# A fold of the layer-1 sums placed behind the pair sums of its slot, in a recommender kernel on one Trainium2 core

## What the reference computes

```
z = einsum('bfe,bge->bfge', x, xk)            # x: embeddings, xk: x itself in layer 0
z = relu(einsum('bcl,oc->bol', z, Ws[i]) + bs[i])
z = sum(z, axis=-1)                           # 16 numbers for a sample
xk = broadcast(z)                             # so layers 1 and 2 need only z of the layer before
```

## Time and profile before

| | before |
|---|---|
| median of 3 runs | 556.3 us (556.26 to 556.32) |
| the profiled execution's own time | 556.66 us |
| its span in the trace | 554.5 us |
| instructions in the span | 17,864 |
| granted TensorE clock | 1.0 of full speed throughout |

### The profile page before, as it was taken

One profiled execution on the slowest core, in us unless ns is written; L12 is line 12 of the kernel. 1 busy time (PEld: TensorE's weight loads), 2 busy tenths in 40 slices (PEclk: granted clock), 3 DMA queues, 4 the chain that ended last, 5 costly groups with the idle time before them and its releaser, 6 DMA issues.

```text
span 554.5 us, 17864 instructions
## 1 busy us (share of the span) xinstructions
PE 525.8 (95%) x7472; PEld 300.4 (54%) x7472; DVE 516.9 (93%) x257; ACT 416.6 (75%) x1208; POOL 459.3 (83%) x533
## 2 busy tenths in 40 slices
PE   2778889999999999999999999999999999999997
PEld 1334544655555565555556555555655555565465
DVE  4799999999999999999999999999999999999763
ACT  3476877878878687887868788786878878687743
POOL 6999898898998989898898989989898999987200
PEclk9999999999999999999999999999999999999999
DMA  3822333332323333232333323233332333332000
GB/s 91 221 77 68 94 90 91 89 83 70 92 83 87 88 82 85 69 98 78 81 90 83 87 69 102 74 86 90 79 87 70 89 85 84 90 82 77 1 2 2
DMA packets 40263, 45.03 MB, mean 81 GB/s; under 512 B 27124, under 2 KB 27508, under 8 KB 40184
## 3 DMA queue, kind: packets, MB, share of 16 engines
q0 software_dynamic: 12288, 33.57, 21.9%
q1 hardware_dynamic: 27896, 10.33, 7.8%
HBM read 42.58 MB, written 1.29 MB: 79 GB/s over the span
## 4 chain that ended last, share of the span: by engine, by line
PE 69%; issue 10%; ACT 9%; DVE 9%; DMA 1%; SPq 1%; POOL 1%; ACTq 0%; DVEq 0%; POOLq 0%
PE sum_ps L693 30%; PE outer_ps L768 9%; PE turn_ps L671 9%; PE outer_ps L799 8%; DVE prods L243 7%; PE sum_ps L708 4%; ACT relu_k L546 4%; PE outer_ps L778 4%; ACT relu L535 2%; PE outer_ps L814 2%; ACT emb_t L508 1%; DMA emb<-tables,rows_sb 1%; ACT h L553 1%; POOL emb L309 1%; PE outer_ps L708 1%
## 5 line engine op out<-in xcount | busy, mean ns | idle before, releaser
L243 DVE TENSOR_TENSOR prods<-turn_ps,emb_t 128x3136 f32<-128x3136 f32 (+3 forms) x126 | 436.5, 3505 | 0.7 <-ACT emb_t L508 0.5
L309 POOL DMA_INDIRECT emb<-tables,rows_sb x256 | 252.2, 985 | 44.4 <-issue 39.1
L693 PE MATMUL sum_ps<-prods,w_sb 128*32 128x272 f32 x4096 | 262.9, 398 | 0.3 <-ACT z_cat L561 0.3
L693 PEld LDWEIGHTS sum_ps<-prods,w_sb 128*32 128x32 f32 x4096 | 122.3, 110 | 130.5 <-issue 51.4
L535 ACT ACTIVATE relu<-sum_ps,bias_twice 128x120 f32<-128x120 f32 x256 | 90.8, 364 | 49.6 <-PE sum_ps L693 48.7
L322 POOL TENSOR_TENSOR prods<-emb_t 128x256 f32<-128x256 f32 x128 | 95.6, 747 | 15.0 <-ACT emb_t L508 12.7
L243 POOL TENSOR_TENSOR prods<-emb_t 128x336 f32<-128x336 f32 (+2 forms) x128 | 104.1, 813 | 2.2
L507 ACT COPY emb_t<-turn_ps 128x512 f32<-128x512 f32 (+1 forms) x126 | 75.7, 600 | 37.1 <-PE turn_ps L671 36.9
L546 ACT ACTIVATE relu_k<-outer_ps,bias_k 128x2048 f32<-128x2048 f32 x44 | 88.0, 2001 | 16.3 <-PE outer_ps L768 16.3
L671 PE MATMUL turn_ps<-ident_sb,emb 128*128 128x128 f32 x502 | 83.1, 288 | 10.7 <-DVE prods L243 8.8
L671 PEld LDWEIGHTS turn_ps<-ident_sb,emb 128*128 128x128 f32 x502 | 52.9, 141 | 63.7 <-issue 39.3
(11 more groups left out here) (78 smaller groups left out, 219.2 us busy)
## 6 DMA issues: line engine op xcount, KB each, us to landing
z_wide<-z_spread SPq DMA_DIRECT2D x29, 256.0 KB
emb<-tables,rows_sb POOLq DMA_INDIRECT x256, 2.9
z_spread<-z_cat SPq DMA_DIRECT2D x116, 2.0 KB
z_spread<-z_wide SPq DMA_DIRECT2D x4, 256.0 KB
w_sb<-w_top SPq DMA_DIRECT2D x1, 512.0 KB
z_cat<-dense_b SPq DMA_DIRECT2D x2, 128.0 KB
w_sb<-w_top SPq DMA_DIRECT2D x1, 256.0 KB
ids_sb<-ids_t SPq DMA_DIRECT2D x1, 129.0 KB, 2.2
```

The lines of the kernel that those rows point to most:

```text
L243: eng.tensor_tensor(out, every, shifted, ALU.mult).then_inc(done, 1)
L309: nc.gpsimd.indirect_dma_start(out=emb[:, k % EMB_RING, t * E:(t + 1) * E], out_offset=None, in_=tables, in_offset=bass.IndirectOffsetOnAx ...
L693: last = nc.tensor.matmul(sum_ps[s * 2 * F:(s + 1) * 2 * F, k % 2, 0:SUM_COLS], w_sb[:, c, odd, :], x[:, c, 2 * s + odd, :, :], start=c == ...
```

## The change

Two things change on TensorE. Every other engine's list stays as it is.

1. `fold(0, g)`, the layer-1 sum over g, stood ahead of the pair sums of slot 8g + 14. It now stands behind them. 14 groups have it there (g = 0 to 13).
2. The wait for z0's copy in slot 8g + 10 stood inside the outer round of that slot, ahead of its last bank (group 0, with no round there, waited ahead of the pair sums). It now stands ahead of the pair sums for every group, 14 of which change. The first pair-sum matmul has a wait of its own (`prods_other`), so this one is a separate instruction.

```diff
@@ sum_pairs
-                    if k == Z0_SUM:
-                        pe.wait_ge(z0_taken, 1)
+                    if (g := group_at(k, Z0_SUM)) is not None:
+                        pe.wait_ge(z0_taken, g + 1)
                     pe.wait_ge(prods_other[k % PRODS_RING], N_OTHER * (k // PRODS_RING + 1))
@@ outer_round
-                    if q == 1 and j == 3 and k == 1:
-                        pe.wait_ge(z0_taken, g + 2)
@@ the loop over slots
-                if (g := group_at(slot, FOLD[0])) is not None and g != PREV:
-                    fold(0, g)
                 if (g := group_at(slot, HIDDEN1)) is not None and slot < STEPS - 1:
                     hidden1(g, h1_banks)
                 sum_pairs(slot)
+                if (g := group_at(slot, FOLD[0])) is not None and g != PREV:
+                    fold(0, g)
```

## The result

The changed kernel takes 564.8 us (564.68 to 564.95) against 556.3 before, a ratio of 1.0153, with a 95% interval of 1.0135 to 1.0170: slower by 8.5 us, or 1.5%. The prediction was 566.0, range 562.0 to 571.0.

A forecast was written before the change was run, and what follows sets the result against it. Two engines are full at once: VectorE binds early, TensorE later, with VectorE having about 0.64 us a period to spare. Group 0's 1.15 plus 13 groups at 0.66 adds 9.7 to 556.3: 566.0 us, range 562.0 to 571.0.

The forecast's parts named there:

- The fold's move on VectorE: Layer 1's reduction on VectorE starts 0.14 us after S15, idle for 1.41 us, with products(16) held behind it.
- TensorE's gains: Slot 14 shrinks by 0.12 us and slot 18's outer round by 0.32, together 0.44 a period.
- The stalls: TensorE waits for VectorE's products: 0.86 us at S16, 0.12 at S18, 0.12 at S20, 1.10 in sum.
- The period: From S20 to the next S20, eight slots grow from 32.23 to 32.89 us, by 0.66.
- The sum: Group 0's 1.15 us plus 0.66 for each of 13 other groups, 8.6, makes 9.7 us over the kernel.
- the work is the same in every group: Every group's period was taken as 32.23 us before, so each of 13 groups costs 0.66.
- Group 0: First group, where VectorE already binds: its reduction goes from 70.07 to 71.22, so everything is 1.15 us later.
- the pipeline's end: It carries the 9.7 us on, as no later wait has slack that long on TensorE.
- Rival 1: Reduction in slot 15 waits below 0.75 us, so TensorE keeps 0.44 a period: 550.1 us; 6 in 100.
- Rival 3: z_wide lands 1.2 us later, delaying slot 17's round: 0.26 a period, 3.6 more, 569.6 us; 9 in 100.
- Rival 4: Separate wait instruction dries TensorE's queue, giving back 0.28 us in slot 18: 2.2 more, 568.2 us; 6 in 100.

The follow-up runs named there:

- e3_reduce_other_data: Changed kernel, but VectorE's layer-1 reduction reads a constant and waits for no fold in groups 0 to 13: 552.1 us against 565.5 for the kernel before.
- e4r_fold_quarter: Changed kernel with layer 1's fold behind the first 8 of 32 pair-sum matmuls, second run: 550.8 us against 556.1 for the kernel before.
- a2_after_again: Changed kernel run again with no edit: 564.5 us, ratio 1.0152 to the kernel before.
- e2r_z0_only: Changed kernel with the fold put back ahead of the pair sums, only z0's wait moved, second run: 551.6 us against 556.1 for the kernel before.
- e4_fold_quarter: Changed kernel with layer 1's fold behind the first 8 of 32 pair-sum matmuls, first run: 560.2 us against 565.5 for the kernel before.

## Why the prediction was right, point by point

- **The fold's move on VectorE.** Predicted: idle for 1.41 us ahead of the reduction, reduction 0.14 after S15. Measured: 1.42 and 0.13. That this is the whole loss is shown by `e3_reduce_other_data`, where the time without the wait falls below that of the kernel before, and by `e4r_fold_quarter` against `a2_after_again`. VectorE's list stands still behind the wait: the products start at 269.98, right behind the reduction. That is the strict order which the Trainium skill states in "TensorE: Matmul & The Clock Gate", section "Architectural detail: the array is 16× 32×32, not 1× 128×128", and the trace agrees.
- **TensorE's gains.** Predicted 0.12 and 0.32 us a period. Measured: 4.31 us for slot 14, as predicted, and 1.15 for the round; `e2r_z0_only` shows the 0.32 by itself and `e4r_fold_quarter` both together.
- **The stalls.** Predicted 0.86 at S16, 0.12 at S18 and 0.12 at S20. Measured: slot 15 takes 4.03 in place of 3.20, so 0.83; slot 17 takes 3.79 in place of 3.64, so 0.15; slot 19 takes 5.27 in place of 5.15, so 0.12. The timeline marks only S16's. From S20, S16 is at 16.62 (predicted 16.64), S17 at 20.07 (20.09) and S18 at 23.86 (23.85).
- **The period.** Predicted 32.89, measured 32.90. TensorE is busy 32.00 us of it and VectorE 31.41, the 0.97 and 0.96 that were predicted.
- **The sum.** Predicted 9.7, measured 8.5, between the medians. The step that was off is "the work is the same in every group". It isn't on TensorE: in every fourth group the output matmuls (L717) stand in slot 15. VectorE's L399, once a period, shows it in the kernel before:

```profile
219.22 0.72 DVE L399 STREAM_TRANSPOSE proj_b<-outer_ps 128x512 f32<-128x512 f32 x1 [0.37 <-PE outer_ps L778]
252.02 0.72 DVE L399 STREAM_TRANSPOSE proj_b<-outer_ps 128x512 f32<-128x512 f32 x1 [0.59 <-PE outer_ps L778]
```

and in the changed kernel, over the same group and the one after it:

```profile
223.76 0.71 DVE L399 STREAM_TRANSPOSE proj_b<-outer_ps 128x512 f32<-128x512 f32 x1
256.66 0.70 DVE L399 STREAM_TRANSPOSE proj_b<-outer_ps 128x512 f32<-128x512 f32 x1
289.56 0.71 DVE L399 STREAM_TRANSPOSE proj_b<-outer_ps 128x512 f32<-128x512 f32 x1
```

  That period was 32.80 us before, not 32.23, and is 32.90 like all others now: the 0.57 of output matmuls lie in TensorE's stall at S16. Three of the 13 groups have them, so 3 x 0.57 = 1.7 comes off, which leaves 8.0. Group 0 cost 1.14 (1.15 predicted, VectorE's L399 at 92.04 against 90.90). By the spans the change cost 562.8 - 554.5 = 8.3. That 8.0 is so close is in part luck, for two more terms nearly cancel. The first two periods were 31.74 and 32.12 before (L399 at 90.90, 122.64 and 154.76) and are 33.01 and 32.90 now: they cost 1.27 and 0.78 in place of 0.66 each, 0.7 more in sum. And the prediction had the pipeline's end carry the whole loss on, but it gives 0.60 back: from the last L399 but one to the last it was 525.07 - 510.98 = 14.09 and is 533.35 - 519.86 = 13.49. VectorE had waited 0.59 for TensorE at 510.98, and waits for nothing at 519.86.
- **Rival 1 (the wait stays under the spare time)** didn't come, but its mechanism is real: `e4r_fold_quarter` is that case, made on purpose, and its 550.8 is near the rival's 550.1.
- **Rival 3 (z_wide late)** didn't come, but by luck more than by the predicted margin of 0.78: the round of slot 17 starts at 277.46, right behind the turn, and the last packet of z_wide's queue lies between 277.0 and 277.2. The last update of its semaphore is at 277.33, 0.13 ahead of the round; before it was 1.60 ahead. SyncE's four DMAs (L283) took 2.61 us to issue there in place of 1.73. In `a2_after_again` four of these rounds start 0.04 to 0.06 behind that update, with the period still 32.9. **Rival 4 (the separate wait)** neither: in slot 18 the pair sums start 282.45 - 281.38 = 1.07 behind the round's start, in slot 17, which has no such wait, 1.08.

## What to carry to other kernels

Before work is moved back on one engine, look at who takes its result and at what stands behind the taker. Here the result was taken 0.07 us after its modelled end by an engine with 0.64 us to spare in a period. Its end came 1.7 us later in the slot (4.38 us after the slot's start in place of 2.66), so that could not be hidden, and the 0.44 us gained on the moving engine were given back more than twice. When two engines are both full, look for a place between the two needs. Here it was better than either end: a quarter of the pair sums ahead of the fold covers the late relu, and the taker still has its result in time.

## What the runs showed of the hardware that I had not expected

The same program took 556.1 and 565.5 or 566.5 us in different groups of runs, at a granted clock within 0.001 of 1.0 each time. The difference shows in the folds, runs of 32 or 64 small matmuls: they complete up to 1 us later than usual, and where pair sums follow, their last starts come later too. It hits kernels through an engine that waits for such a completion: moving the fold alone cost 18 us there, where 11 were expected, and with no wait for layer 1's fold the time was 552.1 and 552.6, within 2 us of what undisturbed matmuls were expected to give. The margin of a quarter of the pair sums was no protection: `e4_fold_quarter` took 560.2 where `e4r_fold_quarter` took 550.8, which is as much lost as in the kernel before.
